# Three-pass weighing and expert projection, other PSUM banks and another order at the first seam, in an eight-stage transformer kernel

## The reference, cut to what matters

```python
x = x + L0_xattn(LN(x), ctx)   # windows of 16 keys, 8 heads of 8
x = x + L0_ffn(LN(x))          # int8-like: gate, up -> silu -> down
x = x + L1_xattn(LN(x), ctx)   # 32 heads of 128, 8 kv heads, rms norm of q and k
x = x + L1_ffn(LN(x))          # mxfp4
x = x + L2_xattn(LN(x), ctx)   # 32 heads of 16
x = x + L2_ffn(LN(x))          # top 16 of 64 experts of rank 16
x = x + L3_xattn(LN(x), ctx)   # 16 heads of 96
x = x + L3_ffn(LN(x))          # 3 bit weights
```

```python
# L1_xattn
probs = softmax(scores); out = einsum('bhgqk,bhkd->bhgqd', probs, v)     # l1_v
# L2_ffn
scores = xf @ Wr.T; top_vals, top_idx = top_k(scores, 16)                # f2_a
h = einsum('nd,krd->nkr', xf, A)                                         # f2_h
out = einsum('nkr,kdr->nd', h * G[:, :, None], B) * 2                    # f2_b, f2_o
```

## Time and profile before

| what | value |
|---|---|
| median of 3 runs | 1628.59 us (1627.83 to 1629.03) |
| profiled execution, own time | 1630.52 us |
| its span, first to last instruction | 1628.7 us |
| mean granted TensorE clock | 0.991 |
| PE busy | 1546.5 us, 95% |
| DVE, ACT, POOL busy | 829.4, 756.0, 519.6 us |
| HBM read, written | 48.77 MB, 2.10 MB |

### The profile page before, as it was taken

One profiled execution on the slowest core, in us unless ns is written; L12 is line 12 of the kernel. 1 busy time (PEld: TensorE's weight loads), 2 busy tenths in 40 slices (PEclk: granted clock), 3 DMA queues, 4 the chain that ended last, 5 costly groups with the idle time before them and its releaser, 6 DMA issues. The chain is left out here.

```text
span 1628.7 us, 26021 instructions
## 1 busy us (share of the span) xinstructions
PE 1546.5 (95%) x9538; PEld 1267.0 (78%) x9538; DVE 829.4 (51%) x1703; ACT 756.0 (46%) x2535; POOL 519.6 (32%) x648
## 2 busy tenths in 40 slices
PE   7899998889999999999999998879999999999998
PEld 6777777778889888888988887655555577888876
DVE  4666666464444545554444436676465321343455
ACT  4545545345454554545455455445333211454552
POOL 7667663222222222222222123334222000123423
PEclk9999998999999999999999999999999999999999
DMA  8000001002010100101010110001000001122101
GB/s 246 8 7 8 8 1 40 27 19 79 27 40 27 40 27 1 40 27 40 27 40 27 40 53 1 1 30 53 37 4 0 24 7 48 40 72 74 51 27 62
DMA packets 44414, 58.05 MB, mean 36 GB/s; under 512 B 25472, under 2 KB 32656, under 8 KB 41472
## 3 DMA queue, kind: packets, MB, share of 16 engines
q1 hardware_dynamic: 43872, 56.05, 10.9%
q10 hardware_dynamic: 352, 0.34, 0.1%
q0 software_dynamic: 64, 0.00, 0.0%
HBM read 48.77 MB, written 2.10 MB: 31 GB/s over the span
## 5 line engine op out<-in xcount | busy, mean ns | idle before, releaser
L1801 ACT ACTIVATE big<-pb 128x128 f32<-128x128 f32 x384 | 106.6, 278 | 311.6 <-PE pb L852 202.7
L2165 POOL TENSOR_TENSOR big<-big 128x512 f32<-128x512 f32 x96 | 100.0, 1042 | 260.5 <-DVE big L1442 260.5
L1852 ACT ACTIVATE big<-pb,big 128x128 f32<-128x128 f32 x384 | 136.1, 368 | 64.7 <-issue 41.6
L1437 DVE TENSOR_REDUCE big<-pb 128x4 f32<-128x512 f32 x96 | 65.9, 686 | 181.3 <-PE pb L891 173.7
L867 PE MATMUL pb<-wkh,CXh 128*128 128x256 f32 x512 | 149.0, 291 | 1.5 <-DVE big L1427 1.5
L2155 POOL TENSOR_SCALAR big<-big 128x6 f32<-128x6 f32 x64 | 13.2, 206 | 419.6 <-ACT big L1801 419.3
L867 PE MATMUL pb<-wkl,CXh 128*128 128x256 f32 x512 | 144.3, 282 | 0.0
L867 PE MATMUL pb<-wkh,CXl 128*128 128x256 f32 x512 | 143.6, 280 | 0.0
L1225 DVE TENSOR_TENSOR X<-X,pb 128x512 f32<-128x512 f32 x128 | 87.0, 680 | 96.3 <-PE pb L1073 41.5
L916 PE MATMUL pb<-woh,oh 128*128 128x512 f32 x256 | 111.8, 437 | 8.3 <-DVE X L1225 5.0
L852 PE MATMUL pb<-wqh,CXh 128*128 128x512 f32 x256 | 102.0, 398 | 5.9 <-DVE big L1407 4.5
(11 more groups left out here) (277 smaller groups left out, 3976.3 us busy)
## 6 DMA issues: line engine op xcount, KB each, us to landing
big<-in_w SPq DMA_DIRECT2D x17, 1024.0 KB, 4.9
big<-in_w SPq DMA_DIRECT2D x24, 256.0 KB, 2.9
big<-in_w SPq DMA_DIRECT2D x8, 512.0 KB, 3.5
o<-o SPq DMA_DIRECT2D x96, 32.0 KB, 1.9
X<-in_x SPq DMA_DIRECT2D x8, 256.0 KB, 4.8
big<-in_cn SPq DMA_DIRECT2D x8, 256.0 KB, 2.7
CXlf<-in_cT SPq DMA_DIRECT2D x8, 256.0 KB, 5.2
big<-in_wa SPq DMA_DIRECT2D x1, 2048.0 KB, 7.9
```

The costliest lines, as they stand in the source:

```text
L1437: v.tensor_reduce(m[j % 2], quarters(bank(p)), AX, MAX, negate=True).then_inc(S.m, 1)
L1801: y = a.activation(sq[i % 2], bank(p)[:, j * width:j * width + 128], ACT.Square, accum_out=ss[i % 2][:, first + j:first + j + 1])
L1852: y = a.activation(e_[:, c], bank(p)[:, c], ACT.Exp, bias=m[j % 2][:, k:k + 1], scale=1.0, accum_out=z[j % 2][:, k:k + 1])
L2165: g.tensor_tensor(quarters(e_), quarters(e_), bc(r[j % 2], 128), MUL).then_inc(*on.to(S.pn))
```

## The change

Matmuls. `l1_v(i)` for 8 <= i < 58 becomes six fp32r matmuls of 256 columns (v high by p high, v low by p high, v high by p low) in place of two f32 calls. ACT writes the values and the transposed probabilities as high parts (`vh`, `pth`, same copies as before with another target), and DVE makes two low parts: `vl` in `l1_n` and `ptl` in a new DVE part of `l1_t`, which stands between `l1_b` and `l1_k`. `f2_h` becomes 24 fp32r matmuls of 512 columns a tile in place of 8 f32 calls. `f2_turn` now makes three copies of the transposed tile: the whole (for `f2_a`, in the neighbouring tile's place), the high and the low one. Its weights `wa` are split by a new stage `f2_split`, eight pieces of 128 x 512, two in each of steps 3 to 6 of `pipe2`.

Banks. `l0_scores(1)` goes from 0 to 1; the gate half of `f0_turn` from 5 to 0 for tiles 0 to 5; `f0_gate` from 6 to 7; `l1_q(2)` from 0 to 7; `l1_k(1)` from 2 to 5.

Order. `f0_split` moves to steps 6 to 8, two pieces in each. `f0_down(5)` now comes ahead of `l1_begin`. `l1_n(0)` moves one step on, behind `l0_out(30)`. The split of the first `wo` moves from `l1_k(3)` to `l1_v(0)`, a step earlier. SP's first loads of layer 3's weights move behind `f2_h(7)`, since `wa`'s high parts now lie there.

```diff
@@ stage_order
-            together(next(att0), (iter([[("l1_begin", 0)]]), 7), (ffn0, 7), (ffn0, 9))
+            together(next(att0), (ffn0, 7), (iter([[("l1_begin", 0)]]), 7), (ffn0, 9))
-        if 7 <= step < 13:
-            order.append(("f0_split", step - 7))
+        if 6 <= step < 9:
+            order.extend([("f0_split", 2 * step - 12), ("f0_split", 2 * step - 11)])
-    for _ in range(3):
+    late = iter(())
+    for step in range(3):
         first, second = next(att0), next(att1)
-        together(first[:7], (ffn0, 7))
+        together(first[:7], (late, 6), (ffn0, 7))
+        if step == 0:
+            late = iter([[second.pop(5)]])
         together(second, (ffn0, 1))
+        if 3 <= step < 7:
+            order.extend(("f2_split", j) for j in range(2 * step - 6, 2 * step - 4))
+        if step == 1:
+            order.append(("l3_first", 0))
@@ psum_uses
-        return [("S", (0,))]
+        return [("S", (1 if i == 1 else 0,))]
-        return [("g", (5,)), ("u", (3,))] if i < NT - 1 else [("g", (4,)), ("u", (6,))]
+        return [("g", (0 if i < NT - 2 else 5,)), ("u", (3,))] if i < NT - 1 else [("g", (4,)), ("u", (6,))]
-    if stage in ("f0_gate", "f0_down") and i < NT - 1:
+    if stage == "f0_down":
         return [("p", (6,))]
-        return [("p", (0,))]
+        return [("p", (7 if i == 2 else 0,))]
-        return [("p", (2 if i < 2 else 1,))]
+        return [("p", ((2, 5)[i] if i < 2 else 1,))]
...
+def in_parts(i):
+    return 8 <= i < 58
@@ tensor_program, l1_v
+                if in_parts(i):
...
+                    for k, (v_, o, pt) in enumerate(((vh, x, pth), (vl, xl, pth), (vh, x, ptl))):
+                        for b in range(2):
+                            a = pe.matmul(bank(p)[:, b * 256:b * 256 + 256], v_[:, o + b * 128:o + b * 128 + 128],
+                                          pt[:, y + b * 256:y + b * 256 + 256], start=(k + b == 0), stop=(k == 2),
+                                          skip_group_check=True)
@@ tensor_program, f2_h
+                on.wait_ge(S.f2l, 8)
-                    for c in range(4):
-                        a = pe.matmul(bank(p), x_rows(LT, c, t), wa[:, c, n * 512:n * 512 + 512],
-                                      start=(c == 0), stop=(c == 3))
+                    for x, low in (CXh, False), (CXh, True), (CXl, False):
+                        for c in range(4):
+                            y = wal[:, 1024 * c + 512 * n:1024 * c + 512 * n + 512] if low else wa_high(c, n)
+                            a = pe.matmul(bank(p), x_rows(x, c, t), y, start=(k == 0), stop=(k == 11))
@@ vector_program
-                if i == 3:
-                    low_parts(wol, woh, wo1[0], 4, S.woh, S.wol, 0)
@@ l1_n
+                    v.tensor_tensor(lo.rearrange("p (g n) -> p g n", g=2), k2[:, :, 128:256],
+                                    hi.bitcast(F32).rearrange("p (g n) -> p g n", g=2), SUB).then_inc(k.free, 1)
@@ l1_t, new
+                    on.wait_ge(S.ph, i - 7)
+                    v.tensor_tensor(ptl[:, k:k + 512], bank(p), pth[:, k:k + 512].bitcast(F32), SUB).then_inc(p.free, 1)
@@ l1_v
+                if i == 0:
+                    low_parts(wol, woh, wo1[0], 4, S.woh, S.wol, 0)
@@ f2_split, new
+                x, hi, lo = f2_parts(j)
+                on.wait_ge(S.f2h, j + 1)
+                v.tensor_tensor(lo, x, hi.bitcast(F32), SUB).then_inc(S.f2l, 1)
@@ scalar_program, turn
+                if kind == "f2":
+                    a.copy(whole_rows(t), quarters(bank(p)))
                 if (kind, t) in SPLIT:
                     a.copy(x_tile(CXh, t), quarters(bank(p))).then_inc(S.xh, 1)
@@ l1_t
+                    a.copy(pth[:, k:k + 512], bank(p)).then_inc(S.ph, 1)
@@ f2_split, new
+                a.copy(hi, x).then_inc(S.f2h, 1)
@@ sync_program
-            def l3_begin(_):
+            def l3_first(_):
                 on.wait_ge(l2_done.full, l2_done.n + 1)
+                read = PSUM["f2_h", 7, 1]
+                on.wait_ge(read.full, read.n + 1)
```

More of the change, by code:

```diff
@@ L328 @@
 STATS, ROWS = layer_norms()
-SPLIT = {k: n for n, k in enumerate((s[:2], i) for s, i in ORDER if s in ("l1_turn", "l3_turn", "f3_turn"))}
+SPLIT = {k: n for n, k in enumerate((s[:2], i) for s, i in ORDER if s in ("l1_turn", "f2_turn", "l3_turn", "f3_turn"))}
 STATS_AT = {n: k for k, n in STATS.items()}
@@ L467, in build_program @@
             here = [0]
+            wah0 = at("wah0", R0 + 7360, 2048)
+            wah1 = at("wah1", R0 + 17504, 1536)
+            wal, wah2 = at("wal", RF + 8, 4096), at("wah2", R0 + 27712, 512)
+        with ExitStack() as places:
+            here = [0]
+            vh, pth = at("vh", R0 + 1848, 1024), at("pth", R0 + 5432, 1024)
+            vl, ptl = at("vl", R0 + 6456, 768), at("ptl", R0 + 27288, 1024)
+        with ExitStack() as places:
+            here = [0]
             w3h = at("w3h", R0 + 8192, 1536)
@@ L600, in build_program @@
         hg, hT = al(1024), al(1024)
[L601 removed]
+        wr = quarters(big[:, R0 + 19040:R0 + 19296])
         al = carve(RF + 8, RW)
[L603 removed]
+        wa = al(4096)
         wb = al(4096).rearrange("p (j n) -> p j n", j=8)
@@ L925, in l1_v @@
                 on.wait_ge(S.v, i + 1)
+                if in_parts(i):
+                    p, turned, made = PSUM["l1_v", i, "p"], PSUM["l1_t", i, "p"], PSUM["l1_k", i, "p"]
+                    on.wait_ge(made.free, made.n + 1)
+                    on.wait_ge(turned.free, turned.n + 1)
+                    on.wait_ge(p.free, p.n)
+                    x, xl, y = 256 * (i % 4), 256 * (i % 3), 512 * (i % 2)
+                    for k, (v_, o, pt) in enumerate(((vh, x, pth), (vl, xl, pth), (vh, x, ptl))):
[3 more added lines that the diff above has]
+                                          skip_group_check=True)
+                    a.then_inc(p.full, 1)
+                    return
                 weigh(PSUM["l1_v", i, "p"], PSUM["l1_t", i, "p"], 128, lambda s: v1[i % 4][:, s * 128:s * 128 + 128],
@@ L1039, in f2_a @@
                 for c in range(4):
-                    a = pe.matmul(bank(p)[:, 0:64], x_rows(LT, c, t), wr[:, c, :],
-                                  start=(c == 0), stop=(c == 3))
+                    a = pe.matmul(bank(p)[:, 0:64], whole_rows(t)[:, c, :], wr[:, c, :], start=(c == 0), stop=(c == 3))
                 a.then_inc(p.full, 1)
             def f2_h(t):
+                on.wait_ge(S.f2l, 8)
                 for n in range(2):
@@ L1412, in l1_n @@
                     on.wait_ge(turned.full, turned.n + 1)
-                v.tensor_tensor(kn[i % 2].rearrange("p (g n) -> p g n", g=2),
-                                bank(k).rearrange("p (g n) -> p g n", g=2)[:, :, 0:128],
-                                bc(rr[i % 2][:, 4:6], 128), MUL).then_inc(k.free, 1)
+                k2 = bank(k).rearrange("p (g n) -> p g n", g=2)
+                y = v.tensor_tensor(kn[i % 2].rearrange("p (g n) -> p g n", g=2), k2[:, :, 0:128],
+                                    bc(rr[i % 2][:, 4:6], 128), MUL)
+                if in_parts(i):
+                    weighed = PSUM["l1_v", i - 3, "p"]
+                    on.wait_ge(weighed.full, weighed.n + 1)
+                    hi, lo = vh[:, 256 * (i % 4):256 * (i % 4) + 256], vl[:, 256 * (i % 3):256 * (i % 3) + 256]
+                    v.tensor_tensor(lo.rearrange("p (g n) -> p g n", g=2), k2[:, :, 128:256],
+                                    hi.bitcast(F32).rearrange("p (g n) -> p g n", g=2), SUB).then_inc(k.free, 1)
+                else:
+                    y.then_inc(k.free, 1)
                 if t == NT - 1 and h < 7:
@@ L1865, in l1_t @@
             def l1_t(i):
+                if in_parts(i):
+                    p, weighed, k = PSUM["l1_t", i, "p"], PSUM["l1_v", i - 2, "p"], 512 * (i % 2)
+                    on.wait_ge(p.full, p.n + 1)
+                    on.wait_ge(weighed.full, weighed.n + 1)
+                    a.copy(pth[:, k:k + 512], bank(p)).then_inc(S.ph, 1)
+                    return
                 turn_probs(PSUM["l1_t", i, "p"], PT1[i % 2], PSUM["l1_v", i - 2, "p"] if i >= 2 else None)
@@ L1943, in l2_t, with f2_split @@
                            bank(p).rearrange("p (x j n) -> p j x n", x=2, j=2)).then_inc(p.free, 1)
+            def f2_split(j):
+                x, hi, _ = f2_parts(j)
+                on.wait_ge(l1_done.full, l1_done.n + 1)
+                on.wait_ge(D.f2, 32)
+                a.copy(hi, x).then_inc(S.f2h, 1)
             def f2_a(t):
@@ L2338, in l2_begin @@
                 load(w2o, d["w2o"], D.w2o)
-                load(wr, d["wr"], D.f2)
+                load(big[:, R0 + 19040:R0 + 19296], d["wr"], D.f2)
             def f2_begin(_):
```

40 lines of the change are left out of this document (29 added, 11 removed).

## The result

| | median us | lowest to highest | runs |
|---|---|---|---|
| before, beside it | 1628.21 | 1627.47 to 1629.03 | 4 |
| changed | 1609.68 | 1606.78 to 1615.97 | 4 |
| changed, once more (e10) | 1608.60 | 1608.12 to 1615.32 | 5 |

The changed kernel takes 0.9891 of the time before, 95% interval 0.9861 to 0.9922: 18.5 us less, where 26.1 less was forecast (1602.5, range 1592 to 1615). Its own executions lie 9 us apart. Those of before lay 1.6 apart here and 7.6 in the first set of experiments. The profiled one is the slowest of its four, 1615.97, with a mean granted clock of 0.985 against 0.988 to 0.991 in the other three. So a second profile of the same kernel was taken (e10, 1608.12, clock 0.991 as in the profile of before).

A forecast was written before the change was run, and what follows sets the result against it. PE's matmul pitches bound layers 1 to 3; in layer 0 and the seam PE waits behind banks and low parts. Layer 0 10.2, seam 9.6, weighing 1.5, expert projection 4.8: 26.1 us off 1628.59 gives 1602.5, range 1592 to 1615.

The forecast's parts named there:

- the 0.8 that I took: Layer 0, tiles 1 to 5: new wait of the gate's transposes for bank 0, held until VectorE's L1311 ends, 0.8 us.
- rival A: Layer 0 tiles and seam: bank 0 takes the wait over, 1.6 us instead of 0.8; 1611 us; chance 0.25 shared with B.
- The quarter that I held back: Layer 0: three quarters of 13.6 us taken, 10.2, as f0's own chain can partly bring a shift of PE back.
- The clock term of 2.4 us: Layer 0, tile 0: full clock lost from 70 to 80 us was to be regained, 2.4 us.
- L798's 3.3 us: Seam: f0_down's read of bank 6 stands behind l1_begin's four low parts; with f0_down first, 3.3 us go.
- 12.8 us of waits: Seam: sum of the five waits addressed, 12.8 us, of which three quarters, 9.6 us, were taken.
- Rival C: Seam: the clock stays at 2.4 GHz and layer 0 gives its full 13.6 us; 1594 us; chance 0.18.
- the chain that I laid out: Layer 1, head ends: late probabilities copy delays low parts, row maximum, L1407 and next l1_q; 0.58 us each, six steps.
- The split was taken at 5 us: Layer 2, f2_split: eight copies and differences of the weights make PE's scores late; 5 us, ends 2.5 and 10.
- Rival B: Layer 2: GpSimd holds four f2_split pieces through a shared port, 7 us in series; 1609.5 us; chance 0.25 shared with A.
- D: Layer 1: weighing waits for ScalarE's copy and VectorE's difference in every unit; slower, 1637.5 us at 0.7 a unit; chance 0.05.
- E: Whole kernel: waits move and matmuls are no shorter; 1628 us within 0.2%; chance 0.02.

The follow-up runs named there:

- e10: The changed kernel once more, with nothing edited, timed beside e9: 1608.60 us; its second profile is an execution of 1608.12 us.
- the first set of experiments: The follow-up runs e1 to e4, each timed in five rounds beside the kernel before, whose median there was 1630.1 us.
- the first: The first profiled execution of the changed kernel, with nothing edited: 1615.97 us.
- e1: Changed kernel with the seam's edits undone (order of l1_begin, l1_n(0) and wo's split; banks of f0_gate(6), l1_q(2), l1_k(1)): 1613.76 us.
- e6: Changed kernel with l1_begin moved ahead of l0_weigh(29), so wq's casts and low parts run before f0_down(5): 1607.10 us.
- e7: Changed kernel with f0_norm(6), whose GpSimd products ran beside wq's low parts, moved behind l1_begin: 1606.73 us.
- e8: Changed kernel with ScalarE's four high parts of wq at a head's end moved from l1_q to l1_k, behind the probabilities' copy: 1605.48 us.
- e2: Changed kernel with layer 1's weighing plain f32 again in every unit: 1609.35 us.
- e3: Changed kernel with the expert projection in one f32 call again, without f2_split or high and low parts of f2's rows: 1611.02 us.
- e5: Changed kernel with each pair of f2_split pieces ahead of l2_e instead of at the step's end: 1601.28 us.
- e9: Changed kernel with both orders: f2_split pairs ahead of l2_e, and wq's high parts in l1_k at a head's end: 1597.73 us.
- e4: Changed kernel with layer 0's edits undone up to tile 5 (f0_split's steps, banks of gate transposes, f0_gate, l0_scores(1)): 1623.80 us.

## Why the prediction was right, and where it was not

*Layer 0: the sum right, in part by luck.* 10.0 and 10.6 against 10.2. At tile 0 the piece of 2.37 us is gone from ahead of the quantisation, the transposes wait 1.02 instead of 3.96, and the clock is 1.00 from 70 to 80 us. The new wait on L1366 was 1.02, three times 1.80, 1.16 and 1.17: above the 0.8 that I took, so rival A's mechanism is there. Tile 0 gave 5.3 of its 6.3 us and the other tiles 4.7 of their 7.3. The quarter that I held back covered this, but it was held back for f0's own chain and not for bank 0. The clock term of 2.4 us didn't last either: up to the fifth mark before, the first and e10 lose the same 5.1 us of full clock. The lowered 6.8 us from 71.8 are gone, but in e10 the clock is lowered for 6.8 us from 103.6, in the first for 3.4 us each from 104.3 and 175.9. Tile 3, as the earlier trace rows:

```profile
207.13 0.69 DVE L1366 TENSOR_TENSOR big<-pb,big 128x512 f32<-128x512 f32 x1
...
207.97 1.06 PE L740 MATMUL pb<-ident,big 128*128 128x128 f32 x8 [1.16 <-DVE big L1366]
...
209.96 1.06 PE L821 MATMUL pb<-big 64*128 64x128 f32 x16
...
211.36 0.37 PE L859 MATMUL pb<-CXh,qgT 128*128 128x256 f32 x1
```

*The seam: the step that failed.* I counted L798's 3.3 us in full, "f0_down now comes first", and asked only what the later waits on f0's chain would leave. The four low parts that f0_down overtook are themselves awaited, by l1_q(0), and behind f0_down they also meet GpSimd's f0 products. PE's waits in the seam, first profile, as the earlier trace rows:

```profile
PE pb L740 <- ACT big L1826: 3.1, 2, 2.5
PE pb L891 <- DVE wql L1306: 3.1, 1, 3.1
PE pb L891 <- DVE big L1460: 1.5, 1, 1.5
PE pb L837 <- DVE big L1435: 1.0, 1, 1.0
```

3.3 became 1.0 + 3.1. The waits of l1_q(2), l1_q(3), wo, f0_gate and l1_k(1) went as forecast, but l1_q(4), which had none before, now waits 1.5 for bank 0 (L1460). That is the second thing that I didn't ask: who uses the bank next. So of 12.8 us of waits 5.6 came back. The transposes of f0's integers (L701 before, L740 now) waited 0.9 us behind f0_turn2(5) before and wait 3.1 now. In all PE's waits in the seam, behind its first mark, fall from 16.6 us to 11.2, by 5.4, and the 5.0 to 6.1 us of e1 fit this. That the sum of the new waits would stay under 3 us was wrong. e6 and e7 show that the 3.1 isn't simply to be had: each moved most of it to the next in the queue.

*The clock.* Rival C asked whether it would stay up in the seam. In e10 it does from 250 to 318 us, in the first profile it doesn't (0.73 from 250 to 275), with equal waits before it. This is worth 4 us between two executions of one kernel and puts the profiled one, 1615.97, just beyond the range. e10 is in the seam what rival C describes, and still gains 7.2 there and not more than 9.6. e1 has the old order, loses no more clock than e10, and its seam is 2.1 shorter than before's, so some 2 us of the 7.2 are clock.

*Layer 1, weighing: right, step by step.* Scores start every 11.10 us instead of 11.25, the 0.15 forecast, though the 0.86 of the earlier trace rows is a weighing of layer 3 (at 1401 us). An end of a head takes 11.71, 0.61 over that (0.58 forecast), and one with a quantisation 13.84, where 12.35 stood before: 1.6 over the saving (1.83 forecast). The end at unit 23, first profile:

```profile
544.40 2.17 ACT L1750 CAST wqh<-big 128x512 fp32r<-128x512 f32 x4
...
546.47 0.58 ACT L1947 CAST pth<-pb 128x512 fp32r<-128x512 f32 x1
...
547.09 0.69 DVE L1514 TENSOR_TENSOR ptl<-pb,pth 128x512 fp32r<-128x512 f32 x1 [2.69 <-ACT pth L1947]
...
547.69 2.49 DVE L1306 TENSOR_TENSOR wql<-big,wqh 128x512 fp32r<-128x512 f32 x4
...
550.11 0.68 DVE L1498 TENSOR_REDUCE big<-pb 128x4 f32<-128x512 f32 x1
...
550.71 0.67 DVE L1460 TENSOR_TENSOR big<-pb,big 128x512 f32<-128x512 f32 x1
```

L1460 starts 550.71 - 546.47 = 4.2 us after the copy, and that copy is behind four casts, the chain that I laid out; in e8 the copy comes first and the four plain ends cost nothing. Four plain ends and two with a quantisation give back 4 x 0.61 + 2 x 1.64 = 5.7 of 7.5 us, which leaves the 1.8 of e2. The scores wait 1.95 and 1.96 (L930), against the 2.2 that 0.93 + 1.25 make.

*Expert projection: matmuls right, the split's clock left out.* 1.33 a tile against 1.2, 10.6 against 9.8. The split was taken at 5 us, all of it waits in the queues, and cost 7.1 to 8.5. The waits were sized about right: 4.4 and 3.9 us. What failed is that the lowered clock was put at nothing: 3.4 and 5.1 us of full clock more than in e3. Not all of that need be the split's, since in the first one lowered stretch begins at 1060.0 and one at 1077.1, ahead of the first piece at 1079.9. But one of 6.8 us, from 1111.2 in the first and 1103.7 in e10, stands behind the waits of the last pieces, and in before, e3, e5 and e9 the clock isn't lowered there. Rival B, the shared port in f2_split, is not what happened, but it wasn't put to the test either: each pair took 1.29 us, and none of the eight pieces had a GpSimd instruction on more than one element per partition beside it.

*D and E.* D fell with e2. E fell with the matmuls' shorter distances and the time.

## What to carry to other kernels

When a wait goes because a reader overtakes other work, name who waits for the work overtaken, what it will now run beside, and who uses the freed bank next. Work put at the end of a step can stand in a ring of several engines even where each engine has room: look for the gap in the ring, here ScalarE's wait for VectorE, and put it there; that was 6 us for a change of order alone. A new wait of PE can cost more than its length when a lowered clock follows, so price both: here some 4 us of waits came with a cost of 7 to 8.5. Compare profiles between equal instructions and look at the granted clock of both before a difference of a few us is given to the change.

## What was not expected of the hardware

One and the same kernel ran from 1606.8 to 1616.0, and one of its stretches of 25 us had the clock at 0.73 in one execution and 1.00 in another. In the undone layer 0 (e4) the executions fell into two groups 6 us apart, with mean granted clocks of 0.988 to 0.991 and of 0.985 to 0.986. What decides between them no run shows. A VectorE instruction on one element per partition (L1439) took 1.23 us with a GpSimd sum of 1.50 beside it (it ended at 264.49, the sum at 264.47), and 0.10 without (e6).
